# Moving row sums, a column-sum remainder and an evacuation in a Flamingo block, and gating the last token tile from x_new with gate sums from GpSimd

## What is computed

```
q1 = fake_quant(layernorm(x));  q2 = fake_quant(ctx)          # 8 bit, scale and zero point given
x  = x + tanh(g_xattn) * (q1 @ q2)
y  = layernorm(x)
logits = y @ W_gate + b_gate;   _, top_idx = top_k(logits, 2)
h  = relu(einsum('bsd,edh->bseh', y, W_e) + b_e)              # only the two chosen experts are computed
x  = x + tanh(g_ffn) * mean of the two chosen h
```

## Time and profile before

| | us |
|---|---|
| median of 3 runs (lowest to highest) | 366.51 (365.27 to 367.09) |
| the profiled execution's own time | 366.18 |
| its span | 364.4 |
| busy: PE, DVE, ACT, POOL | 323.4, 229.5, 133.7, 112.5 |
| mean granted TensorE clock | 0.966 |

### The profile page before, as it was taken

The page is one execution under the profiler, slowest core; times in us unless marked ns, Lnnn a source line. Parts: engine busy times, 40 slices in busy tenths (PEclk is TensorE's granted clock), DMA queues, the critical chain, the costliest instruction groups (busy, mean ns, idle before and its releaser), DMA issues.

```text
span 364.4 us, 7003 instructions
## 1 busy us (share of the span) xinstructions
PE 323.4 (89%) x1732; PEld 251.3 (69%) x1740; DVE 229.5 (63%) x361; ACT 133.7 (37%) x113; POOL 112.5 (31%) x131
## 2 busy tenths in 40 slices
PE   0579787998877999999999999999999999999960
PEld 0224364677844888888888888888888888888840
DVE  2898998886987973298949434933239434943220
ACT  3865876544503621267335114401135114411100
POOL 3552445000012314154128333233314332333310
PEclk9999999999569999999999999999999999999995
DMA  6999577320595997499998974995239943454233
GB/s 229 414 409 385 182 298 304 149 98 19 206 333 179 412 402 161 112 296 376 362 358 224 400 162 122 335 341 117 38 115 310 353 109 114 114 115 103 38 89 58
DMA packets 23004, 81.46 MB, mean 224 GB/s; under 512 B 3152, under 2 KB 3152, under 8 KB 22992
## 3 DMA queue, kind: packets, MB, share of 16 engines
q1 hardware_dynamic: 16656, 58.76, 42.0%
q0 software_dynamic: 6192, 22.55, 25.8%
q10 hardware_dynamic: 144, 0.01, 0.0%
HBM read 62.43 MB, written 18.87 MB: 223 GB/s over the span
## 4 chain that ended last, share of the span: by engine, by line
PE 73%; DVE 16%; DMA 3%; issue 3%; POOL 1%; ACT 1%; POOLq 0%; DVEq 0%; ACTq 0%
PE ps L1214 60%; PE ps_y L1190 5%; PE ps L1021 4%; DVE st L698 4%; DVE xt L762 2%; DMA y_rows<-y_scratch,idx 2%; DMA par<-in_small_dram 2%; PE ps_s L1073 1%; DVE onehot L823 1%; PE ps_y L1048 1%; PE ps L1028 1%; DVE mv L700 1%; DVE lnv L720 1%; DVE u8c L744 1%; POOL q L408 1%
## 5 line engine op out<-in xcount | busy, mean ns | idle before, releaser
L1214 PE MATMUL ps<-w_hi,yT_hi 128*128 x320 | 126.5, 395 | 0.5 <-DVE yT_lo L950 0.5
L1214 PE MATMUL ps<-w_hi,yT_lo 128*128 x320 | 124.8, 390 | 0.0
L1214 PE MATMUL ps<-w_lo,yT_hi 128*128 x320 | 124.5, 389 | 0.0
L829 DVE TENSOR_TENSOR w_lo<-stage,w_hi 128x2048 f32 (+1 forms) x32 | 72.0, 2286 | 11.3 <-ACT w_hi L633 9.6
L482 POOL DMA_INDIRECT out_dram<-res,sidx x20 | 32.7, 1634 | 133.9 <-DVE res L984 119.0
L633 ACT ACTIVATE w_hi<-stage 128x2048 f32 x28 | 52.5, 1911 | 57.1 <-PE ps L1214 37.8
L981 DVE TENSOR_TENSOR res<-ps,bias 128x512 f32<-128x512 f32 x40 | 27.5, 688 | 67.8 <-issue 36.2
L1214 PEld LDWEIGHTS ps<-w_hi,yT_hi 128*128 128x128 f32 x320 | 60.1, 188 | 12.7 <-issue 0.9
L1214 PEld LDWEIGHTS ps<-w_hi,yT_lo 128*128 128x128 f32 x320 | 60.1, 188 | 12.7
L1214 PEld LDWEIGHTS ps<-w_lo,yT_hi 128*128 128x128 f32 x320 | 60.2, 188 | 11.8
L620 ACT ACTIVATE yT_hi<-ps_y 128x1024 fp32r<-128x1024 f32 x21 | 21.4, 1021 | 114.4 <-PE ps_y L1190 114.4
(11 more groups left out here) (156 smaller groups left out, 261.6 us busy)
## 6 DMA issues: line engine op xcount, KB each, us to landing
stage<-in_L_ffn_W_e_dram SPq DMA_DIRECT2D x32, 1024.0 KB, 7.5
stage<-in_ctx_dram SPq DMA_DIRECT2D x16, 512.0 KB, 11.7
xt<-in_x_dram SPq DMA_DIRECT2D x8, 512.0 KB, 11.4
y_scratch<-y SPq DMA_DIRECT2D x8, 512.0 KB, 3.0
out_dram<-xt SPq DMA_DIRECT2D x8, 512.0 KB, 3.1
bias<-in_L_ffn_b_e_dram SPq DMA_DIRECT2D x8, 512.0 KB, 4.3
y_rows<-y_scratch,gidx POOLq DMA_INDIRECT x22, 5.5
out_dram<-res,sidx POOLq DMA_INDIRECT x20, 6.3
```

Source lines behind the costliest of these rows:

```text
L829: dve.tensor_tensor(w_lo[:, dst], stage[:, CK * c:CK * (c + 1), :].rearrange("p k h -> p (k h)"), w_hi[:, dst].bitcast(f32), ALU.subtract) ...
L1214: last = pe.matmul(ps[q][:, h * 512:(h + 1) * 512], lhs[q][:, k, :], w[:, bass.ds(woff + k * D + h * 512, 512)], start=(k == 0 and lhs is ...
```

## The change

It does six things. (1) `rowsums(0)` on PE moves from behind the second batch's column sums to ahead of them, and `read_rowsums(0)` on DVE to ahead of `centre_q1(5)`; since the row sums stand in ps_s, `transpose_q1(5)` now waits until they are read. (2) `keep_colsum_lo(1)` on DVE moves ahead of two `scales` and a `normalise`. (3) ACT evacuates yT of tile 0 before q1T of tile 4. (4) y of tile 7 is still made, for the store to DRAM, but by ACT. Its gating no longer uses it: PE transposes x_new of tile 7 itself and multiplies it with W_gate, and since y = AA * x + BB the logits are AA * (x W_gate) + BB * (column sums of W_gate) + bias. (5) These column sums come from three small additions on POOL (`wpart`, from eight k-tiles to one) and one fp32 matmul with ones (`gate_sums`). (6) The groups of the selection become tiles 0 to 3 and 4 to 7; the one-hots of the first group are made before the second selection, and `rowsums(1)` follows `gate(7)`.

```diff
         rows_in = (ps_s[:, 0:TPB], ps[1][:, 512:512 + TPB])
-        gates_in = (ps_s[:, NT:NT + TPB * E], ps_g[:, 0:TPB * E], ps[0][:, 0:E])
-        GROUPS = ((0, TPB), (TPB, NT - 1), (NT - 1, NT))
+        gates_in = (ps_s[:, NT:NT + TPB * E], ps_g[:, 0:TPB * E])
+        wsum_in = ps_g[:, TPB * E:(TPB + 1) * E]
+        GROUPS = ((0, TPB), (TPB, NT))
...
         POOL_Q1, DVE_Q1 = (0, 1, 2, 6), (3, 4, 5, 7)
-        ACT_Y, DVE_Y = (1, 2), (0, 3, 4, 5, 6, 7)
+        ACT_Y, DVE_Y = (1, 2, 7), (0, 3, 4, 5, 6)
...
             pool.memset(eps[:, :], EPS)
+            pool.memset(ones_f[:, :], 1.0)
             pool.memset(pick[:, :], 0.0)
...
                       allow_small_or_imprecise_dtypes=True).then_inc(s_iota, 1)
+            pool.wait_ge(s_wg, 16)
+            pool.tensor_tensor(wpart[:, 0:4, :], wg[:, 0:4, :], wg[:, 4:8, :], ALU.add).then_inc(s_wt, 1)
+            pool.wait_ge(s_wt, 1)
+            pool.tensor_tensor(wpart[:, 4:6, :], wpart[:, 0:2, :], wpart[:, 2:4, :], ALU.add).then_inc(s_wt, 1)
+            pool.wait_ge(s_wt, 2)
+            pool.tensor_tensor(wpart[:, 6, :], wpart[:, 4, :], wpart[:, 5, :], ALU.add).then_inc(s_wt, 1)
             add_rowsum(0)
...
-                act.wait_ge(s_ab[1], i // 2 + 1)
+                act.wait_ge(s_ab[1], 6 if i == NT - 1 else i // 2 + 1)
                 if i >= 2:
...
             quantise_ctx(15)
+            keep_yT(0)
             keep_q1T(4)
-            keep_yT(0)
             keep_q1T(5)
...
             std(1, 7, 1, 6)
+            normalise(7)
             keep_yT(7)
...
                 dve.wait_ge(s_gate, e)
-                dve.tensor_tensor(u(lg), gates_in[g][:, 0:n * E].rearrange("p (i e) -> p i e", e=E),
-                                  bg.unsqueeze(1).to_broadcast([P, n, E]), ALU.add).then_inc(s_lg, 1)
+                m = n - 1 if e == NT else n
+                if e == NT:
+                    link(dve.scalar_tensor_tensor(shift[:, :], wsum_in, lnv[:, 1, BB, NT - 1:NT], bg, ALU.mult, ALU.add))
+                    dve.scalar_tensor_tensor(lg[:, m, :], gates_in[g][:, m * E:n * E], lnv[:, 1, AA, NT - 1:NT],
+                                             shift[:, :], ALU.mult, ALU.add)
+                dve.tensor_tensor(lg[:, 0:m, :], gates_in[g][:, 0:m * E].rearrange("p (i e) -> p i e", e=E),
+                                  bg.unsqueeze(1).to_broadcast([P, m, E]), ALU.add).then_inc(s_lg, 1)
                 dve.wait_ge(s_lg, g + 1)
...
             x_new(3)
+            read_rowsums(0)
             centre_q1(5)
...
             x_stats(7)
-            read_rowsums(0)
+            keep_colsum_lo(1)
             scales(1, 2, 2, 2)
...
             scales(0, 6, 2, 4)
-            keep_colsum_lo(1)
             x_new(4)
...
             scales(1, 7, 1, 6)
-            normalise(7)
             positions(0)
             slot_matrix(0)
-            select(1)
-            read_rowsums(1)
             dve.wait_ge(s_iota, 1)
...
                 make_onehot(i)
+            select(1)
+            read_rowsums(1)
             positions(1)
             slot_matrix(1)
-            select(2)
-            for i in range(TPB, NT - 1):
+            for i in range(TPB, NT):
                 make_onehot(i)
-            positions(2)
-            slot_matrix(2)
-            make_onehot(NT - 1)
...
             def transpose_y(i):
-                wait_y(pe, i)
+
+                if i == NT - 1:
+                    pe.wait_ge(s_xn, NT)
+                else:
+                    wait_y(pe, i)
                 if i >= 1:
                     pe.wait_ge(s_ye, i)
+                rows = xt[:, i, :] if i == NT - 1 else y[i % 2][:, :]
                 for k in range(KT):
-                    last = pe.transpose(ps_y[:, k, :], y[i % 2][:, k * P:(k + 1) * P], ident_f[:, :])
+                    last = pe.transpose(ps_y[:, k, :], rows[:, k * P:(k + 1) * P], ident_f[:, :])
                 last.then_inc(s_yt, 1)
+
+            def gate_sums():
+
+                pe.wait_ge(s_wt, 3)
+                pe.matmul(wsum_in, ones_f[:, :], wpart[:, KT - 2, :], start=True, stop=True)
...
                     pe.wait_ge(s_wg, 16)
-                    pe.wait_ge(s_rs, 1)
+                    pe.wait_ge(s_qe, 6)
                 if i == TPB:
                     pe.wait_ge(s_qe, NT)
-                if i == NT - 1:
-                    pe.wait_ge(s_xn, NT)
                 pe.wait_ge(s_ye, i + 1)
-                g = i // TPB + i // (NT - 1)
+                g = i // TPB
                 into = gates_in[g][:, (i - GROUPS[g][0]) * E:(i - GROUPS[g][0] + 1) * E]
...
                 fold(i)
+            rowsums(0)
             pe.wait_ge(s_xn, 3)
...
             column_sums(KT + 4, KT + 6)
+            pe.wait_ge(s_rs, 1)
             transpose_q1(5)
...
             column_sums(KT + 6, 2 * KT)
-            pe.wait_ge(s_qe, 6)
-            rowsums(0)
             attend_after(4)
...
             counts(0)
+            transpose_y(7)
+            gate_sums()
             gate(6)
-            transpose_y(7)
-            pe.wait_ge(s_xn, NT - 1)
+            gate(7)
+            pe.wait_ge(s_xn, NT)
             rowsums(1)
-            counts(1)
-            gate(7)
             pe.wait_ge(s_xn, NT - 1)
...
             place_rows(0)
-            counts(2)
+            counts(1)
             place_rows(1)
-            place_rows(2)
             keep_clock(20)
```

More of the change, by code:

```diff
@@ L90, in flamingo_gated_moe @@
         tri = at("tri", [P, E + 1, E], f32, YT + 10 * KB + 256)
+        ones_f = at("ones_f", [P, P], f32, WLO + 8 * KB)
+        wpart = at("wpart", [P, KT - 1, E], f32, WLO + 9 * KB)
         iota_pe = at("iota_pe", [P, P, E], bf16, WLO + 32 * KB)
@@ L116, in flamingo_gated_moe @@
         lg = sb("lg", [P, TPB, E], f32)
+        shift = sb("shift", [P, E], f32)
         rank = sb("rank", [P, TPB, E], f32)
@@ L197, in flamingo_gated_moe @@
         s_gate = sem("gating_in_psum")
+        s_wt = sem("gate_sum_step")
         s_lg = sem("logits_read")
```

## The result

The changed kernel is slower: 369.59 us in the median of 20 runs (367.25 to 372.3), against 366.26 for the kernel before; ratio 1.0099, 95% interval 1.0077 to 1.0122. I had predicted 364.2 (362.0 to 367.0) and given 0.08 to "slower". The profiled execution took 371.07 us, 1.5 above the median of the twenty; that of the kernel before took 366.18, close to its median.

A forecast was written before the change was run, and what follows sets the result against it. PE was taken to bound the kernel (73% of the chain), its expert loop unchanged but starting earlier: tokens 3.1 us earlier, less 0.8 for a slower first gather, give 2.3 off the 366.5 median, 364.2 us (362.0 to 367.0).

The forecast's parts named there:

- The first gather: First token gather ahead of the expert loop: SP's transfers come 5.2 us closer, adding 0 to 3.0 us, taken as 0.8.
- the first case: First gather beside a quarter of expert 1's weights, as in the kernel before: 5.75 us, so added cost 0.
- The upper row, 8.8: Profile row of a gather amid weight loads, 8.8 us, used as the upper case: 3.0 us added to the first gather.
- The rival with 0.08: Before the expert loop: gather takes 8.8, PE idles 4.8 us, clock falls, costing about 2.2 more: 368.6 us, chance 0.08.
- The front: Attention of batch 1 up to tile 7's new x: that comes 2.1 us earlier, at 83.0.
- The tail: From tile 7's new x through last gating and second selection to the tokens' copy: tokens at 101.7, 3.1 us earlier.

The follow-up runs named there:

- the front alone: Kernel before plus only the three moves ahead of routing (first batch's row sums, column sums' remainder, yT copy of tile 0): 365.29 us, ratio 0.9957.
- the tail alone: Changed kernel with the three moves ahead of routing undone: 371.96 us, ratio 1.0123 against the kernel before.
- second experiment: Changed kernel, with the first quarter of expert 1's weights issued only after both gathers have landed: 366.86 us, ratio 1.0012.
- the bridge: Changed kernel with second batch's row sums made and read early, plus five unread PE matmuls ahead of `gate(4)`: 362.95 us, ratio 0.9899.
- both edits: Changed kernel with early second-batch row sums, five unread matmuls ahead of `gate(4)`, and ACT copying yT of tile 7 before making its y: 361.87 us, 0.9867.
- the first four experiments: Changed kernel with early second-batch row sums (363.62 us), delayed expert weights (366.86), or 50 clock-keeping matmuls (370.04); kernel before with late row sums (369.68).

## Why the prediction was wrong

**The step that failed is "The first gather"**: I bounded its added cost by 0 to 3.0 us and took 0.8, since it was "nearest to the first case". Measured, it was 4.6 in the profile of the changed kernel and 2.5 when late row sums were put into the kernel before. I had the distance right (I said 5.2 us closer; it was 3.9 + 1.45 = 5.3), and drew the wrong price from it. Its parts were off by 1.8 and 1.7 us, and the distance was not, because the late new x of tile 7, below, moved the stores and the gather alike. In the profile the forecast gain of 2.3 us became a loss of 5.0: 3.8 of the difference lie in this term, 1.7 in the later tokens and 1.8 in the fallen clock. The row I leaned on was a gather issued when the stores had landed and one bias load and 1 MB of weights were left. Moved 5.3 us closer, it met the last stores, both bias loads and the weights, and for 4.5 us nothing of it moved at all. The upper row, 8.8, was a gather beside weights alone and was no upper bound. By issue time against SP's first store, the profiles give: 12.0 us behind it 4.5, 10.4 behind it 5.8 (5.3 with the front alone), 6.7 behind it 8.2, and 5.0 behind it, with the weights in the queue, 8.4 to 11.3 (10.4 in the changed kernel, 11.3 with the tail alone).

The Trainium skill ("DMA: Bandwidth & Descriptors", "Queues, rings and completion order") has each DMA engine go round-robin between its queues packet by packet, and the prediction read from it that nothing would be added. The runs refute that reading: 4.6 us were added, and in the profile SP's queue moved 1.32 MB while the gather's moved none. Whether the gather's packets already stood in their queue in that stretch, the trace does not show, so it does not speak against the rule itself.

**Then the clock.** The rival with 0.08 (the first gather takes 8.8, PE idles 4.8 us, and the clock falls: 368.6) is the mechanism that happened, with 10.4, 5.8 and 369.6. That its number comes within 1 us is partly luck: it had the tokens 3.1 us earlier, and they were 1.4. I priced the fall at 2.2; the profile has 1.8 up to the loop, and the runs with 38 clock-keeping matmuls put it near 2.3. What I got wrong is its chance.

**The front.** `fold(4)` at 56.27 (56.5 forecast), the additions on POOL 0.25, 0.22 and 0.20 us (I took 0.9 in all), its pair of adds ending at 54.5, `scales(1, 2)` unstalled, quantising from 59.32 (59.2), `gate(4)` at 78.04 (77.8): all as worked out. The step after it failed: "PE then has no wait left up to `fold(7)`, so tile 7's new x is 2.1 earlier, 83.0". PE indeed had no wait there (0.22 us in all), but the sum took its work at the upper clock, and I did not ask what PE's new wait of 1.09 us for ACT, ahead of `gate(4)`, could do to that. In the profile of the changed kernel the clock fell at 79.9, behind that wait and the gating, and the transposes (1.92) and the second half of tile 7's attention (2.33 for seven matmuls) ran at 1.2 GHz: new x of tile 7 at 84.94 instead of 83.0. Where the clock held (second experiment, the bridge, both edits) it was 83.14 to 83.21. The second experiment has the same wait and held its clock, so the wait alone does not decide, and what does stays open. The front alone gives 1.6 us on average.

**The tail.** From new x of tile 7 to the tokens 18.4 us (84.94 to 103.38), against 18.7 forecast and 19.8 before. A gating of 3.58 at the low clock (3.5), DVE's wait of 1.88 ahead of the selection (1.9): right. The prediction had `read_rowsums(1)` in its sums twice, as 0.2 us on DVE and as the reason why the stores come 2.1 us later. It saw the chain and took its price for small; this lateness was the change's true cost.

What stays open: how much of the gather's time is the bias loads' and how much the stores', what holds its first packet back, and why the same order gave 8.4 in two profiles and 10.4 in another. None of it was tried apart.

## What to carry to other kernels

When an edit shifts two chains against each other, price the transfers that meet, not only the engines: here an instruction of 0.28 us that nobody on the critical path needs released 4 MB of transfers. Later in the kernel before it cost 4 us, and earlier in the changed kernel, with the sums on PE moved too, it gave about 6; earlier in the kernel before it gave nothing, and in that profile the gather was covered. Start bulk transfers that nothing waits for as early as their data allow, so that they are through when the short, urgent one goes. And after making an engine faster, look for the wait that it newly has: here the clock fell behind a new wait of 1.1 us on PE in most profiles, and that took back what the front had won.

## What the runs showed of the hardware

Whether the clock falls differs between executions of the same order, and this seems to be much of the spread between runs. Of the four profiles whose code is that of the changed kernel up to 98 us, it fell at about 80 us in three and held in one, that of the second experiment. In the session of the first four experiments the kernel before has two clumps, 364.8 to 366.0 and 366.9 to 367.5, and one run of 492.7; in the first measurement, of 20 runs, three lie between them. Up to 60 us its code is the same as in the kernel with earlier row sums, and both wait for the remainder of the column sums to 60.2. In that kernel's profile (first row) the clock fell behind the wait, in the one of before (second row) it did not:

```profile
62.00:64.00 2.00, 2.00 (x8) 1.04 (x7) 1.97 (x4) 1.26 (x2) 1.88 (x2) 0.50 0.40 164
```

```profile
62.00:64.00 2.00, 2.00 (x15) 1.29 (x12) 1.97 (x4) 2.00 (x2) 1.93 (x2) 1.00 0.39 158
```

New x of tile 5 then came at 69.14 instead of 67.55, and everything behind it 1.6 us later, which is near the distance of the clumps. A single profile of this kernel is uncertain by 1.6 us at that one wait, and a forecast should be held against many runs.
